# A fused attention and mixture-of-experts kernel on 8 cores: which PSUM banks its projections and its router use

## The reference

```
xn   = layernorm(x)
q, k = rotary(xn @ wq.T), rotary(xn @ wk.T);   v = xn @ wv.T
attn = (softmax(q @ k.T / 32) @ v) @ wo.T
out  = sum over 2 shared experts of (silu(xn @ wg) * (xn @ wu)) @ wd       # middle width 512
p    = softmax(xn @ router_w)                                              # 16 experts
comb = the two largest p of a token, divided by their sum, 0 elsewhere
out += sum over 16 experts of (silu(xn @ wg_e) * (xn @ wu_e) * comb_e) @ wd_e   # width 256
result = x + attn + out
```

## Time and profile before

| | us |
|---|---|
| timed executions | 4426.1, 4841.71, 4857.33 (median 4841.71) |
| profiled execution, own time | 4386.11 |
| its span on the slowest core (core 1) | 4384.6 |
| spans of the 8 cores | 4329.6 to 4384.6 |
| mean granted TensorE clock of the cores | 0.895 to 0.910 |
| TensorE busy | 3551.2 (81%) |
| VectorE busy | 1472.7 (34%) |
| ScalarE busy | 606.1 (14%) |

### The profile page before, as it was taken

One profiled execution on the slowest core, in us unless ns is written; L12 is line 12 of the kernel. 1 busy time (PEld: TensorE's weight loads), 2 busy tenths in 40 slices (PEclk: granted clock), 3 DMA queues, 4 the chain that ended last, 5 costly groups with the idle time before them and its releaser, 6 DMA issues.

```text
span 4384.6 us, 49454 instructions; the slowest of 8 cores (4329.6 to 4384.6 us)
## 1 busy us (share of the span) xinstructions
PE 3551.2 (81%) x15904; PEld 1530.7 (35%) x15904; DVE 1472.7 (34%) x3681; ACT 606.1 (14%) x1507; POOL 23.6 (1%) x50
## 2 busy tenths in 40 slices
PE   3555453787878787878787869999999999999999
PEld 1111121333333333333333324444444444444433
DVE  3555100334343443444434423232323232323231
ACT  2222110111111111111111101010101010101010
POOL 0000000000000000000000000000000000000000
PEclk8777776889998898999898979999999999999987
DMA  4444899101010101010101064443444444444332
GB/s 118 135 133 128 151 133 134 52 6 54 6 53 6 54 6 54 6 53 6 53 6 44 6 160 147 139 149 140 144 142 147 141 143 140 150 145 146 125 125 87
DMA packets 110219, 412.59 MB, mean 94 GB/s; under 512 B 13312, under 2 KB 21760, under 8 KB 87312
## 3 DMA queue, kind: packets, MB, share of 16 engines
q1 hardware_dynamic: 105520, 359.06, 24.4%
q0 software_dynamic: 3296, 41.98, 7.2%
q10 hardware_dynamic: 1152, 8.39, 0.5%
HBM read 415.57 MB, written 58.85 MB: 108 GB/s over the span
## 4 chain that ended last, share of the span: by engine, by line
PE 70%; DMA 10%; DVE 9%; issue 6%; ACT 4%; DVEq 1%; SPq 0%; ACTq 0%; POOLq 0%
PE pb L101 70%; DMA wdr_bf<-wdr 6%; DVE d_sc L101 2%; DMA f_wd<-wdr_bf 2%; ACT d_P L101 2%; DVE b_st L101 1%; DVE d_OT L101 1%; DVE b_kswp L101 1%; DMA d_stl<-stab 1%; ACT d_sc L101 1%; DMA b_x<-x 1%; DVE d_qfm L101 1%; DMA c_wvT<-wvT 1%; DMA f_wgu<-wgu_bf 1%; DVE b_xntok L101 1%
## 5 line engine op out<-in xcount | busy, mean ns | idle before, releaser
L101 PE MATMUL pb<-f_xnt,f_wgu 128*128 128x512 bf16 x4096 | 933.5, 388 | 27.2 <-DMA f_xnt<-xn_sp 18.8
L101 PE MATMUL pb<-Vs,d_PT 128*128 128x512 bf16 x2048 | 546.3, 405 | 91.3 <-DVE d_PT L101 91.3
L101 PEld LDWEIGHTS pb<-f_xnt,f_wgu 128*128 128x128 bf16 x4096 | 397.8, 99 | 532.0 <-issue 134.0
L101 PE MATMUL pb<-f_wd,f_h 128*128 128x512 bf16 x2048 | 472.7, 391 | 28.3 <-DMA f_wd<-wdr_bf 13.1
L101 PE MATMUL pb<-Kfm,d_qfm 128*128 128x512 bf16 x2048 | 463.8, 389 | 11.7 <-ACT d_cbt L101 11.7
L101 DVE SCALAR_TENSOR_TENSOR f_uu<-pb,f_cb 128x512 bf16<-128x512 f32 x256 | 177.1, 692 | 590.6 <-PE pb L101 590.6
L101 DVE CAST d_PT<-pb 128x128 bf16<-128x128 f32 x1024 | 289.8, 291 | 228.0 <-PE pb L101 228.0
L101 ACT ACTIVATE f_sg<-pb 128x512 bf16<-128x512 f32 x256 | 152.9, 597 | 1340.8 <-PE pb L101 1249.7
L101 PEld LDWEIGHTS pb<-f_wd,f_h 128*128 128x128 bf16 x2048 | 198.7, 100 | 302.2 <-issue 118.1
L101 PEld LDWEIGHTS pb<-Kfm,d_qfm 128*128 128x128 bf16 x2048 | 202.5, 100 | 263.6 <-issue 37.2
L101 PEld LDWEIGHTS pb<-Vs,d_PT 128*128 128x128 bf16 x2048 | 171.0, 103 | 239.8 <-issue 123.9
(11 more groups left out here) (89 smaller groups left out, 2324.3 us busy)
## 6 DMA issues: line engine op xcount, KB each, us to landing
f_wgu<-wgu_bf SPq DMA_DIRECT2D x126, 1024.0 KB, 4.9
f_wd<-wdr_bf SPq DMA_DIRECT2D x128, 512.0 KB, 3.3
b_x<-x SPq DMA_DIRECT2D x32, 512.0 KB, 4.6
b_ct<-ctab SPq DMA_DIRECT2D x64, 256.0 KB, 3.0
b_stl<-stab SPq DMA_DIRECT2D x64, 256.0 KB, 3.3
wgu_bf<-wgu POOLq DMA_DIRECT2D x16, 1024.0 KB, 31.6
d_ct<-ctab SPq DMA_DIRECT2D x64, 256.0 KB, 2.7
d_stl<-stab SPq DMA_DIRECT2D x64, 256.0 KB, 2.8
```

The lines of the kernel that those rows point to most:

```text
L101: inst = getattr(eng, meth)(*args, **kw)
```

## The change

The banks of four groups of matmuls are numbered differently. No instruction is added, taken away or moved; the waits that `mm_group` derives from the banks follow. K's projection rotates through banks 2, 3, 6, 7, V's through 0 to 3, Q's through 6, 7, 2, 3, and the router's logits use banks 0 and 1 in place of 0 to 3.

```
@@ phase_b1: K projection
-                    bank = 2 + (j % 2)
+                    bank = (2, 3, 6, 7)[j % 4]
@@ phase_b2: V projection
                 for h in range(2):
-                    bank = h
+                    bank = (kc % 2) * 2 + h
@@ phase_d: router logits
             for s4 in range(4):
                 q0 = s4 * 128
+                rb = s4 % 2
                 trt = self.mm_group(
-                    s4, self.pb[s4][:, 0:NE],
+                    rb, self.pb[rb][:, 0:NE],
...
                 tlg = P.op("V", "tensor_copy",
                            lg4[:, s4 * NE:(s4 + 1) * NE],
-                           self.pb[s4][:, 0:NE],
-                           waits=self.pbf[s4].rd() + [self._rt_s_prev[s4]],
+                           self.pb[rb][:, 0:NE],
+                           waits=self.pbf[rb].rd() + [self._rt_s_prev[s4]],
                            inc="V")
-                self.bank_read(s4, self.mark("V", tlg))
+                self.bank_read(rb, self.mark("V", tlg))
@@ phase_d: Q projection
-                bank = 6 + (j % 2)
+                bank = (6, 7, 2, 3)[j % 4]
```

## The result

The changed kernel takes 1.0105 times as long as the one before (95% interval 1.0091 to 1.0118): 1.05% slower. In that comparison its ten timed executions have a median of 4403.03 us and the ten of the kernel before one of 4392.01. Executions in which the cores of a die ran at a lower granted clock are left out of every ratio here; the undisturbed ones of this comparison lie from 4392.95 to 4404.52 us after and from 4352.11 to 4357.91 us before, so the difference is about 46 us. The profiled execution took 4403.7 us.

The account below looks back on a forecast made before the run. TensorE, busy 81% of the span, was taken as the engine whose standstills decide. K, Q, V 0 and router 7 x 5.9 + 0.4 = 42 us, added to 4386.11, gave 4428 us, 1.0% slower; range 4390 to 4900 us.

Parts of the forecast that it names:

- K, Q and V: nothing: Projections of K, Q and V: an older wait already covers the banks' new freedom; cost and gain 0.
- (a): Router, seven later tiles: VectorE's first logit copy still comes about 4.98 us after the router matmuls start.
- (b): Router: third group restarts at 993.6, so Q's projection starts at 994.0 instead of 989.1, 4.9 us late.
- (c): Q's projection after idle: runs at 1.2 GHz, 5.48 us in place of 3.61; first rotary copy 6.1 us late.
- (d): Q's second rotary step: takes 4.06 us in place of 4.26, returning 0.2, leaving 5.9 us per tile.
- (e): First query tile: no chain ahead of the logit copies, so the router's new wait costs only 0.4 us.
- The sum: Whole kernel: K, Q, V 0, router 7 x 5.9 + 0.4 = 42 us; 4386.11 + 42 = 4428 us.
- slower by over 2%: Rival: clock also falls more often inside the tiles' scores, 50 us more, 4478 us; chance 0.05.
- within 2%: Outcome class for the kernel's time, holding the forecast and two rivals, taken as indistinguishable from no change; chance 0.91.
- Absorbed: Rival, tile start: VectorE limits it anyway, so the late projection costs nothing, 4386 us; chance 0.12.
- The low clock lasts: Rival: all 16 projection matmuls at 1.2 GHz, six further steps 0.2 us longer each; 62 us, 4448; chance 0.08.
- The banks free the projections: Rival: waits ahead of K's and Q's swaps are for banks, 206 us could go; 4222 us, 3.7% faster; chance 0.04.

Follow-up runs that it names:

- the rotations alone: K, V and Q rotations of the change, router left on banks 0 to 3, against the kernel before; no ratio, executions left 4334.48 to 4353.32 us.
- the filled wait: Whole change plus 20 thrown-away 128x512 matmuls ahead of the third router group in tiles 2 to 8, against the kernel before: 1.0076.
- the fast one: Separate reader records for Q's rotary halves, fourth block's comb chain moved later, against the kernel before: 0.9813 with new banks, 0.982 with old.
- both edits and the old banks: Kernel before with separate reader records for Q's rotary halves and each tile's fourth comb chain moved behind the next tile's first scores: 0.982.

## Why the prediction was right or wrong

- *K, Q and V: nothing.* Borne out by the unchanged waits after the change and by the rotations alone. The older wait of the swap covers the bank's wait in both projections.
- *The router's wait, (a) and (b).* Right. The copies came 4.96 us after the router (4.98 in the sum), the third group started 5.28 us after the first (5.3), with 4.74 us of idle time. The projection started 5.72 us after the router on core 5 (5.7 in the sum).
- *The clock, (c).* Right in kind, shown by the filled wait. The size differs by tile: the first swap comes 10.5 to 11.8 us after the router. I took one length, 5.48 us, from one start at the low level. That the first rotary copy comes after 11.5 us on average, where the sum has 11.6, is in part luck.
- *What is given back, (d).* Right: the second step takes 4.06 us.
- *The first tile, (e).* 0.4 us as worked out: the projection starts 1.22 us after the router on core 5, where it was 0.85. The tile's scores do not start later (36.1 us after the router against 37.7 on that core), and the cores differ by more than this term.
- *The sum.* 42 us forecast for the router; the tiles' starts give 7 x 5.9 = 41, and the whole is 46 us by the timed executions. The rest lies mainly between the scores and the next router: 186.9 us a tile after against 186.1 before on core 5, 5 us in seven tiles. The work there is the same. The sum has no term for it, and the prediction says "Nothing downstream of Q's projection changes"; the rival "slower by over 2%" named a lower clock there, at 50 us. See the last section.
- *Where it failed: the base of the sum and what I made of the executions.* The 42 us were added to 4386.11, the profiled execution, whose two slowest cores had lost 35 to 40 us in the experts' stage, core 1 at a granted clock of 0.96 where core 5 had 0.99. The base should have been about 4354, the median of the executions before that the ratio counts, and 4354 + 46 = 4400. The measured change is 46 us, so the term of 42 was right to 4 us; what put 4428 some 25 us above the measured time is the base. I had not compared the cores by stage; the table's spans of 4329.6 to 4384.6 us and clocks of 0.895 to 0.910 were the sign. Beside that I set 4428 against a median of 4841.71 shown for the kernel before. Read against that median the number says 8.5% faster, though the text says 1.0% slower; a forecast has to be stated as a ratio to one base. The upper end of 4900 came from the same place and said nothing of the change. That the range of 4390 to 4900 holds the 4403 is owed to its width: its lower end was meant as the case without a loss, and the 4352 to 4358 us of the kernel before lie below it.
- *Where it failed: "about 2% is what a measurement can tell from no change".* The interval is 0.14% to each side. The 1.05% are over seven times that. I had the size and the sign, and gave 0.91 to "within 2%" without saying that 0.79 of it was a loss that a measurement would show.
- *Rivals.* "Absorbed" is out: the tile's scores start 5.9 us later. "The low clock lasts" is out: the second step is 4.06 us with a short swap. "Slower by over 2%" is out by the measured 1.05%. "The banks free the projections" is out: the waits ahead of the swaps are 122.4 and 86.8 us. The rule of the Trainium skill (page "Perfetto Trace Analysis", section "Matmul Optimizations") to use all 8 banks gave no gain that the time of the slowest core shows here, neither with the slow rotary nor with the fast one.

## What to carry to other kernels

Before banks or buffers are added, look at what the engine waits for by name: here the waits were for the copy that makes the swap's input and, in Q's projection, behind it for one record of readers that two halves of a tile shared, and no bank could help. When a bank is reused, the price is not the length of the copy that empties it but the queue ahead of that copy; 14 small operations stood ahead of a copy of 0.17 us. And a few microseconds of idle time on TensorE are to be priced with the slow matmuls behind them.

## What the runs showed of the hardware that was not expected

A kernel with 20 useless matmuls of 128x512 in each of seven waits is faster than the same kernel without them (1.0076 against 1.0105 of the kernel before). The projection behind the wait then runs at a granted clock of 1.00 in place of 0.50.

The same idle time does not always end at the same clock. In the third tile the product with V starts behind 2.85 us of idle time in both kernels; first before (core 0), then after:

```profile
1259.02 0.59 PE L101 MATMUL pb<-Vs,d_PT 128*128 128x512 bf16 x2 [2.85 <-DVE d_PT L101]
```

```profile
1275.94 0.86 PE L101 MATMUL pb<-Vs,d_PT 128*128 128x512 bf16 x2 [2.85 <-DVE d_PT L101]
1276.69 1.06 PE L101 MATMUL pb<-Vs,d_PT 128*128 128x512 bf16 x2
```

The first two matmuls take 0.59 us in the one and 0.86 in the other, where the next two take 1.06. From the scores to the next router the windows view gives 184.05 us at a clock of 0.90 before and 186.24 at 0.89 after, for the same instructions (columns as in the earlier trace rows):

```profile
1238.60:1422.65 184.05, 154.22 (x726) 70.01 (x741) 68.06 (x238) 25.09 (x77) 0.00 (x0) 0.90 0.03 12
```

```profile
1256.71:1442.95 186.24, 156.31 (x726) 70.93 (x741) 68.15 (x238) 25.08 (x77) 0.00 (x0) 0.89 0.03 11
```

The same is found within one kernel. With both edits and the old banks, core 0 takes 184.82 us at a clock of 0.91 for its fourth tile and 188.24 to 188.38 at 0.89 for the other five of tiles 2 to 7. So a tile can take 2 to 4 us more or less without any change in its work, with the clock as the only difference that the rows show. That this is where the last 5 us of the loss come from is argued from these rows, not shown: no run moved a tile in time and left all else as it was.
